# New instruction orders for four engines in the three batch loops of a fused four-layer kernel

## What is computed

```python
x = x + L0_ffn(L0_cond(x, cond_8))     # low-rank adapted linear; layer norm, attention and MoE with gates per token
x = x + L1_ffn(L1_cond(x, onehot))     # one Silu expert per batch; 16 routed GELU experts, layer norm
x = x + L2_ffn(L2_cond(x, logits))     # two chosen GELU skills and a shared one; soft MoE with 2048 slots:
    D = softmax(logits over slots of an expert); C = softmax(logits over experts)
    X_tilde = clip(einsum('tznp,tzd->npd', D, x)); X_tilde = tanh(layernorm(X_tilde))
    Y = einsum('tznp,npH->tzH', C, X_tilde @ expert_w + expert_b)
x = x + L3_ffn(L3_cond(x, cond_8))     # masked linear; rotary attention, RMS norm, grouped experts, RMS norm
return x
```

## Time and profile before

| | us |
|---|---|
| median of 3 runs | 1416.57 |
| profiled execution | 1420.51 |
| its span, first to last instruction | 1418.7 |
| PE busy | 1128.4 (80%) |
| PE weight loads busy | 802.2 (57%) |
| DVE busy | 764.0 (54%) |
| ACT busy | 497.6 (35%) |
| POOL busy | 213.2 (15%) |
| mean granted clock of TensorE | 0.895 of 2.4 GHz |

### The profile page before, as it was taken

How to read it: one execution, slowest core, us unless ns; L and a number is a source line. 1 busy time by engine, 2 the same in 40 slices (tenths; PEclk the granted TensorE clock), 3 DMA queues, 4 the chain that set the end, 5 groups by cost and what they waited for, 6 DMA issues and landing times.

```text
span 1418.7 us, 17725 instructions
## 1 busy us (share of the span) xinstructions
PE 1128.4 (80%) x6726; PEld 802.2 (57%) x6726; DVE 764.0 (54%) x1667; ACT 497.6 (35%) x740; POOL 213.2 (15%) x176
## 2 busy tenths in 40 slices
...
DMA packets 13035, 34.96 MB, mean 25 GB/s; under 512 B 3680, under 2 KB 7440, under 8 KB 12179
## 3 DMA queue, kind: packets, MB, share of 16 engines
...
q0 software_dynamic: 32, 0.01, 0.0%
...
## 4 chain that ended last, share of the span: by engine, by line
PE 39%; issue 32%; DVE 12%; ACT 7%; POOLq 4%; DVEq 2%; POOL 1%; ACTq 0%; DMA 0%
PE ps L1080 4%; PE ps L805 4%; PE ps L1213 3%; PE ps L1067 3%; PE ps L815 3%; PE ps L1140 2%; PE ps L862 2%; PE ps L839 2%; PE ps L1156 2%; PE ps L1013 1%; PE ps L1120 1%; DVE arena L1865 1%; POOLq L2025 1%; ACT L1264 1%; ACT L1281 1%
## 5 line engine op out<-in xcount | busy, mean ns | idle before, releaser
L1418 ACT ACTIVATE arena<-ps 128x2048 f32<-128x2048 f32 x32 | 60.1, 1879 | 106.4 <-PE ps L1144 106.4
L1865 DVE TENSOR_REDUCE arena<-ps 128x8 f32<-128x2048 f32 x32 | 73.2, 2287 | 28.1 <-PE ps L1120 28.1
L1013 PE MATMUL ps<-arena 128*128 128x128 f32 x512 | 74.4, 306 | 12.5 <-DVE xacc L1783 6.5
L987 PE MATMUL ps<-arena,uR 128*128 128x512 f32 x128 | 73.7, 659 | 12.6 <-ACT arena L1365 12.2
L1013 PEld LDWEIGHTS ps<-arena 128*128 128x128 f32 x512 | 69.7, 217 | 19.9 <-issue 11.4
L1067 PE MATMUL ps<-uR,arena 128*128 128x256 f32 x256 | 74.0, 387 | 1.4 <-DVE arena L1820 1.4
L1080 PE MATMUL ps<-arena 128*128 128x256 f32 x256 | 64.6, 403 | 10.7 <-DVE arena L1846 10.7
L1213 PE MATMUL ps<-arena 128*128 128x512 f32 x128 | 66.2, 665 | 3.1 <-DVE xacc L1936 2.0
L1391 ACT ACTIVATE arena<-ps 128x512 f32<-128x512 f32 x64 | 38.3, 599 | 78.1 <-PE ps L1068 78.1
L1080 PEld LDWEIGHTS ps<-arena 128*128 128x128 f32 x256 | 50.0, 201 | 26.5 <-DVE arena L1846 12.7
L1770 DVE TENSOR_REDUCE arena<-arena 128x32 f32<-128x1024 f32 x32 | 39.0, 1219 | 48.0 <-ACT arena L1365 48.0
...
## 6 DMA issues: line engine op xcount, KB each, us to landing
...
```

Source lines behind the costliest of these rows:

```text
L987: mm(o, uR[:, b, k * P:(k + 1) * P], phiC[:, col:col + 512], start=True, stop=False)
L1013: last = mm(high[:, 2, t * P:(t + 1) * P], eD[h][:, k, col:col + P], uT[u][:, k, :], start=k == 0, stop=k == 1)
L1418: av(pexp[:, t, gp].rearrange("p c h t -> p (c h t)"), scores[:, :, :].rearrange("p c t -> p (c t)"), ACT.Exp, scale=SCALE3).then_inc(s.sc ...
L1865: V.tensor_reduce(nm[:, k, :, 2 * gp:2 * gp + 2], scores[:, :, :].rearrange("p c (h t) -> p c h t", h=2), X, ALU.max, negate=True).then_in ...
```

## The change

Only the order lists differ. Every list has the same words as before, no word is lost or new, and no step's code is touched. The lists of SP (both loops' loads and the stores) and that of POOL in stage B are the same word for word. In the others steps change places, within a batch and between batches: all of PE's, ACT's and DVE's lists of A and B from about the second batch on, a few neighbours in POOL's lists of A and D, and in D mostly PE's list, with a few words of ACT's and DVE's.

In the new lists of stage A the pattern repeats every two batches, in those of stage B every batch (before: every batch in A and every three in B). The core of the diff, with one stretch of each list that the text speaks of:

```diff
 ORDER_A "PE"
-    SPR1.2 GTR0.4 VT.3 COND.5 SPR0.4 AT.3 MOE.2 O1.3 QK.4 NT1.3 UG0.2 SC.4 NT0.5 LOG1.3 MH0.3 LOG0.5 UG1.2 MH1.3
-    DN.2 PT.4 GTR1.3 L1G.2 SPR1.3 GTR0.5 VT.4 COND.6 SPR0.5 AT.4 MOE.3 O1.4 QK.5 NT1.4 UG0.3 SC.5 NT0.6 LOG1.4
-    O1.6 QK.7 NT1.6 UG0.5 SC.7 LOG1.6 MH0.6 UG1.5 MH1.6 DN.5 PT.7 GTR1.6 L1G.5 SPR1.6 VT.7 AT.7 MOE.6 O1.7 UG0.6
+    L1G.2 GTR1.3 MH1.3 SC.4 VT.4 SPR1.3 PT.4 GTR0.5 AT.4 COND.6 MOE.3 SPR0.5 UG0.3 O1.4 UG1.3 QK.5 DN.3 NT1.4
+    SC.5 L1G.3 NT0.6 LOG1.4 VT.5 PT.5 MH0.4 AT.5 MH1.4 LOG0.6 GTR1.4 SPR1.4 O1.5 MOE.4 GTR0.6 NT1.5 UG0.4 COND.7
+    SPR0.6 LOG1.5 UG1.4 MH0.5 MH1.5 QK.6 DN.4 GTR1.5 SC.6 L1G.4 SPR1.5 NT0.7 VT.6 PT.6 LOG0.7 MOE.5 AT.6 GTR0.7
+    UG0.5 SPR0.7 O1.6 UG1.5 QK.7 DN.5 NT1.6 SC.7 L1G.5 LOG1.6 VT.7 PT.7 MH0.6 AT.7 MH1.6 GTR1.6 SPR1.6 O1.7
 ORDER_A "ACT"
-    GU1.2 DN.1 GTR1.2 GX0.4 PTC.3 GTR0.4 LX.1 VC.3 RW0.4 RW1.4 QKC.4 AF1.3 SI0.2 AF0.5 EX.4 GU0.3 GX1.3 SI1.2
-    GU1.3 DN.2 GTR1.3 GX0.5 PTC.4 GTR0.5 LX.2 VC.4 RW0.5 RW1.5 QKC.5 AF1.4 SI0.3 AF0.6 EX.5 GU0.4 GX1.4 SI1.3
+    QKC.4 GTR1.3 LX.2 GU1.3 EX.4 VC.4 PTC.4 GTR0.5 RW0.5 SI0.3 RW1.5 SI1.3 QKC.5 DN.3 AF1.4 AF0.6 LX.3 EX.5
+    GX1.4 VC.5 PTC.5 GU0.4 GU1.4 GTR1.4 GX0.6 GTR0.6 AF1.5 SI0.4 RW0.6 RW1.6 SI1.4 GU0.5 GX1.5 GU1.5 QKC.6 DN.4
 ORDER_A "DVE"
-    GB1.3 GA0.5 GE1.3 HM1.2 GB0.5 GE0.5 LA.2 S8M0.3 L1.2 S8M1.3 S8B0.4 S8A0.5 S8B1.4 S8A1.5 X1.3 LN0.6 LN1.4
+    LN1.4 HM1.3 NH1.4 MXA.5 LA.3 GA1.4 GB1.4 L1.3 GE1.4 S8B0.5 S8B1.5 GA0.6 GB0.6 S8M0.4 S8M1.4 GE0.6 LN1.5
 ORDER_B "PE"
-    MT1.4 SG0.5 SH1.4 SU0.5 SG1.5 LG2.4 SU1.5 SG2.5 XT0.4 SG3.5 MT2.4 BC1.6 SU2.5 SG4.5 SH2.4 SU3.5 SG5.5 LG3.4
-    UC.7 MT3.6 UT.7 SH3.6 MC.6 LG0.7 XT2.6 MT0.7 XT3.6 SH0.7 LG1.7 MT1.7 SH1.7 LG2.7 XT0.7 MT2.7 XT1.7 SH2.7
+    SG0.5 HID0.6 LG2.3 SU0.5 XT0.3 HID1.6 MT2.3 SG1.5 XT1.3 SH2.3 SU1.5 SG2.5 BC0.6 SU2.5 LG3.3 SG3.5 BC1.6
+    SG4.5 MT3.3 SG5.5 SH3.3 Z.6 SU3.5 LG0.4 XT2.3 SU4.5 MC.3 MT0.4 SU5.5 SH0.4 XT3.3 LG1.4 UC.5 MT1.4 ZT.6 UT.5
+    SH3.5 SU3.7 MC.5 SU4.7 LG0.6 XT2.5 MT0.6 SU5.7 SH0.6 XT3.5 LG1.6 UC.7 MT1.6 UT.7 SH1.6 LG2.6 XT0.6 MT2.6
 ORDER_B "ACT"
-    UC.4 MT3.3 SH3.3 MC.3 UT.4 MT0.4 SH0.4 ZT.5 HID0.6 HID1.6 MT1.4 SG0.5 SH1.4 SG1.5 SG2.5 SG3.5 MT2.4 SG4.5
+    SH1.3 SG0.5 HID0.6 HID1.6 MT2.3 SG1.5 SH2.3 SG2.5 SG3.5 SG4.5 MT3.3 SG5.5 SH3.3 MC.3 MT0.4 SH0.4 UC.5 ZT.6
 ORDER_B "DVE"
-    XT2.3 ZN.5 XT3.3 SH0.4 LG1.4 X2.5 BC0.6 SU0.5 SH1.4 LG2.4 SU1.5 XT0.4 BC1.6 SU2.5 SU3.5 SH2.4 LG3.4 SU4.5
+    SH2.3 LG3.3 BC1.6 MC.3 SU2.5 SH3.3 SU3.5 LG0.4 SU4.5 XT2.3 LN.6 SU5.5 SH0.4 XT3.3 LG1.4 ZN.6 X2.6 SH1.4
 ORDER_D "PE"
-    X5T.3 CL5.5 CL6.5 G3.3 MX2.4 CL7.5 FF0.3 MX3.4 CSUM.5 FF1.3 SO.3 NM.4 TS0.4 RT0.3 TS1.4 Y0.5 RT1.3 Y1.5
-    TS2.4 Y2.5 Y3.5 TS3.4 S.5 OUT.3 AV0.4 V.5 AV1.4 Q.5 K.5 AVT.4 CL0.6 CL1.6 SAT.4 MX0.5 CL2.6 WO.4 CL3.6 MX1.5
+    X5T.3 CL5.5 G3.3 CL6.5 MX2.4 CL7.5 FF0.3 MX3.4 CSUM.5 FF1.3 SO.3 NM.4 TS0.4 RT0.3 TS1.4 Y0.5 RT1.3 TS2.4
+    Y1.5 Y2.5 TS3.4 Y3.5 OUT.3 S.5 AV0.4 V.5 AV1.4 Q.5 K.5 AVT.4 CL0.6 CL1.6 SAT.4 CL2.6 MX0.5 WO.4 CL3.6 CL4.6
 ORDER_D "ACT"
-    X5T.0 G3.0 FF0.0 NM.1 TS0.1 FF1.0 TS1.1 TS2.1 TS3.1 SQ2.0 S.2 V.2 AV0.1 AV1.1 CL0.3 CL1.3 SAT.1 CL2.3 CL3.3
+    CL7.2 G3.0 FF0.0 FF1.0 NM.1 TS0.1 TS1.1 TS2.1 TS3.1 SQ2.0 S.2 V.2 AV0.1 CL0.3 AV1.1 SAT.1 CL1.3 SQ1.1 CL2.3
 ORDER_D "DVE"
-    RR.4 X3.6 FIN.4 OUT.4 RQ.6 RK.6 SA.5 MX0.6 X5.5 MX1.6 G3.5 MX2.6 CSUM.7 FH0.5 MX3.6 GE.5 NM.6 FH1.5 REC.7
+    RR.4 FIN.4 X3.6 OUT.4 RQ.6 RK.6 SA.5 MX0.6 X5.5 MX1.6 G3.5 MX2.6 CSUM.7 FH0.5 MX3.6 GE.5 NM.6 FH1.5 REC.7
```

More of the change, by code:

```diff
@@ L129 @@
[L129 to L131 removed]
+    QK.1 NT1.0 NT0.2 VT.1 SC.1 LOG1.0 MH0.0 PT.1 MH1.0 LOG0.2 AT.1 GTR1.0 SPR1.0 O1.1 MOE.0 GTR0.2 NT1.1 UG0.0
+    COND.3 SPR0.2 LOG1.1 UG1.0 MH0.1 MH1.1 QK.2 DN.0 GTR1.1 SC.2 L1G.0 SPR1.1 NT0.3 VT.2 PT.2 LOG0.3 MOE.1 AT.2
@@ L152 @@
     "PE": """
[L153 to L162, removed]
@@ L190 @@
-    SH0.6 LG1.6 SU2.7 SU3.7 SH1.6 LG2.6 SU4.7 XT0.6 SU5.7 SH2.6 LG3.6 XT1.6 MC.6 SH3.6 LG0.7 XT2.6 XT3.6 SH0.7
+    HID0.0 BC0.0 HID1.0 BC1.0 Z.0 ZT.0 HID0.1 BC0.1 SG0.0 HID1.1 SU0.0 BC1.1 SG1.0 SU1.0 Z.1 SG2.0 SU2.0 SG3.0
+    SU3.0 ZT.1 SG4.0 SU4.0 SG5.0 SU5.0 UC.0 UT.0 LG0.0 SG0.1 HID0.2 SU0.1 SG1.1 MT0.0 BC0.2 SU1.1 SH0.0 HID1.2
+    BC1.2 SG2.1 SU2.1 LG1.0 SG3.1 MT1.0 SG4.1 SH1.0 SU3.1 Z.2 LG2.0 SG5.1 XT0.0 SU4.1 MT2.0 ZT.2 SH2.0 SU5.1
+    XT1.0 LG3.0 UC.1 MT3.0 UT.1 SG0.2 SH3.0 SU0.2 HID0.3 MC.0 SG1.2 BC0.3 SU1.2 LG0.1 HID1.3 XT2.0 SG2.2 MT0.1
@@ new lines @@
+    BC1.3 SH0.1 SU2.2 XT3.0 SG3.2 LG1.1 SU3.2 Z.3 SG4.2 MT1.1 SU4.2 SG5.2 SH1.1 SU5.2 ZT.3 UC.2 LG2.1 UT.2 SG0.3
+    HID0.4 XT0.1 MT2.1 SG1.3 SU0.3 HID1.4 SH2.1 SU1.3 SG2.3 XT1.1 LG3.1 SU2.3 BC0.4 SG3.3 SG4.3 MT3.1 BC1.4
+    SG5.3 SH3.1 Z.4 SU3.3 LG0.2 XT2.1 SU4.3 MC.1 MT0.2 SU5.3 SH0.2 XT3.1 LG1.2 UC.3 MT1.2 ZT.4 UT.3 SH1.2 SG0.4
+    HID0.5 LG2.2 SU0.4 XT0.2 HID1.5 MT2.2 SG1.4 XT1.2 SH2.2 SU1.4 SG2.4 BC0.5 SU2.4 LG3.2 SG3.4 BC1.5 SG4.4
+    MT3.2 SG5.4 SH3.2 Z.5 SU3.4 LG0.3 XT2.2 SU4.4 MC.2 MT0.3 SU5.4 SH0.3 XT3.2 LG1.3 UC.4 MT1.3 ZT.5 UT.4 SH1.3
```

130 lines of the change are left out of this document (66 added, 64 removed).

## The result

The changed kernel takes 1336.89 us (median of four runs, 1333.51 to 1342.84), the kernel before 1415.68 beside it; the ratio is 0.9447, 95% interval 0.9406 to 0.9489: 5.5% faster. Forecast were 1352 us and a range of 1325 to 1394. The profiled execution took 1342.84 us, the longest of the four (span 1341.0, mean granted clock 0.916 against 0.895).

The account below looks back on a forecast made before the run. Each loop was taken as TensorE work plus gaps, A's gap bringing a slow clock. Savings of 42 + 17 + 6 = 65 us took the profiled 1420.5 to 1355.5, and the median's 3.9 lower gave 1352; range 1325 to 1394.

Parts of the forecast that it names:

- The loads, counted: ScalarE table loads in all three loops: by the table rule 24 fewer, 104 in all, 30.8 us of ScalarE.
- A, -42: Stage A: QK hides the chain before DN, closing the 4.8 us gap; period 43.2 to 33 us, 42 us less.
- B, -17: Stage B: 46.7 us a batch instead of 51.9, 31 us less, minus the end's cost and an allowance: 17 less.
- the price of the lag: Stage B's end: two softmax rounds move behind the last UC, taking 21.2 us there; 10.6 come back net.
- for batches 1 to 3 ... I allow 3: Stage B: 3 us allowed as loss for early batches that follow no pattern in the new list.
- D, -6: Stage D: earlier G3 and OUT before S shorten TensorE's waits, 6 us less in all.
- 1.0 us a batch, six times: Stage D's steady part: 0.4 us from earlier G3 and 0.6 us from OUT before S, in six batches.
- G3 earlier lets MX2 be read 0.4 us earlier: Stage D: MX2, then MX3 and the sum TensorE waits for, come about 0.4 us earlier.
- Only the loads are gained: Whole kernel: other waits replace the gap before DN and the slow clock stays; 1397 us, chance 0.13.
- The stalls of B and D go as well: Stages B and D also lose their stalls, the lag costing nothing; 90 us less, 1327 us, chance 0.08.
- The slower case: In-order DVE waits hold stage B's period at 51.9 while SPR1 and MH0 limit A; 1427 us, chance 0.04.
- the fourth: Whole kernel: loads are placed by another rule, the orders only shift the waits; 1415 us, chance 0.03.

Follow-up runs that it names:

- the second profile: Profile from rerunning the changed kernel with no edit; median 1336.6 us, stage A 354.0 us.
- only A new: Kernel before with only stage A's lists new, those of B and D old: 1370.02 us, ratio 0.9659.
- no loads: Kernel before with Tanh in place of every Gelu and Silu of the three loops, so ScalarE never changes tables there: 1327.6 us.
- the DN experiment: Changed kernel with DN.0 to DN.5 on TensorE moved up directly behind UG1 of the same batch, loads unchanged: 1363.44 us, ratio 0.9629.

## Why the prediction was right, and where it missed

**The loads, counted.** Right: 104, and line by line as walked. The place was right too: a load hidden by ScalarE's own wait costs nothing (seventeen in B: 0), one in the chain costs its length or more (six in A: 1.3 to 1.9 us each). One sentence was wrong in size: "in B and D most loads run while ScalarE would wait anyway". How many do was not counted, but the loads there cost the old orders 24 and 10 us.

**A, -42.** Measured -41.2, and -45.6 by the second profile. The steps of the cause held: QK (for DN.2 MH and LOG) hides SI1 and HM1, no wait before DN is above 1.1 us, 164.4 us from DN.0 to DN.5, and 52.2 against 47.2 us from there to DN.7, so the 5 us given back were there. Two details did not: the period is not even (28.0, 33.2, 35.4, 40.5, 27.3, since batches alternate), and the clock isn't 1.00 throughout. Stretches of 3.4 us at half clock are left. In two of these, windows of PE busy all the time:

```profile
149.00:152.40 3.40, 3.40 (x18) 3.40 (x17) 2.44 (x24) 0.34 (x3) 0.73 (x2) 0.52 0.01 2
217.30:220.70 3.40, 3.40 (x18) 3.40 (x18) 2.44 (x23) 1.75 (x7) 0.33 (x1) 0.52 0.01 3
```

Ahead of each stands DN and then 2.4 to 3.2 us of small products (L769, L820, L821, L885, L774, L777: mostly 128 columns down to one), and then a wait of 0.84 us in one case and of 0.13 in the other. Each costs about 1.7 us. Whether the small products are the cause was not tried. That the sum met is in part luck. From DN.0 to DN.5 TensorE is busy for 159.1 us and idle for 5.3; the prediction had 159 of work at the full clock and 6.5 of waits. But some 3.4 of the 159.1 are slow clock, so the work itself was overestimated by as much, and the waits by 1.2. And the whole gain depends on the loads: without them the old order of A is the shorter one.

**B, -17.** Measured -27.3: the walk of the new list was right and a size was off. The steady period came as predicted (46.65 against 46.7), and so did the price of the lag (20.5 us more behind the last UC, where 21.2 was put) and its credit: the two rounds are missing between UC.1 and UC.2, an interval of 35.5, 11.1 below the steady one, where 10.6 was put. What failed is the rest of "for batches 1 to 3 ... I allow 3". The interval from UC.2 is 44.9 and the last 43.9 (no X2 work of a next batch stands in it), together 4.5 below the steady one, where the allowance had them 3 above; UC.0 to UC.1 gave 1.0 more, the tail 0.7 and the two rounds 0.5. That is 9.7 of the 10.3 us missed. A term of which no row spoke had been put on the safe side. The prediction also gave the better period to the order alone. Without loads the old order takes 48.9 us from one UC to the next in place of 51.9, so 3 of the 5.2 us a batch are what the loads cost it.

**D, -6.** Measured -9.2, by another way, so that the size came near is luck. The step that failed is "1.0 us a batch, six times". From OUT.1 to OUT.5 the new lists take 56.3 us a batch in the first profile, the old ones 56.6 in two profiles and 56.1 in two others (only A new, and no loads): no gain clear of that spread. The 0.6 us of AV0 went, but the wait before CSUM stayed at 1.5 us, and filling it moved it on. "G3 earlier lets MX2 be read 0.4 us earlier" failed as a step: VectorE's list has the sum behind MX2's reduction and ahead of FF1's input, and that list sets the moment. The gain lies at the start: OUT.0 to OUT.1 fell from 58.6 to 58.9 us to 53.7, in all profiles. Ahead of OUT.0 the first two profiles differ by 3.3 us, but with the old lists this part also took 157.7 us (only A new), 0.6 more than with the new ones. The two loads of FF1.0 and TS1.1 stood in the chain there in the kernel before; how much of the 3.3 us is theirs no run shows, since putting them back put them behind other waits. The prediction had priced them at 2.6 and only as an end of the range.

**The rivals.** "Only the loads are gained" (1397) falls with the DN experiment, since the loads stayed and over half of A's gain went. "The stalls of B and D go as well" (1327) was nearer in B than the forecast's 17. The slower case needed SPR1 and MH0 to be late by 2 us or more. Between DN.0 and DN.5 SPR (L794) waits 0.5 us once and MH (L851) 0.3; behind DN.5 one SPR does wait 3.0 us, at 316.3 us, among the last batches' steps. The table rule was what it said, so the fourth falls with the counts.

Two of the three errors had one sign: B by 10, D by 3, A by less than 1 the other way. With them 1352 becomes 1339; the other 2 us are that the profiled execution lies 6.0 us above the median, where before it lay 3.9 above.
